# Taking the maximum of the next head's score pair first in each group of VectorE's attention stream

## The reference, cut to what matters

```python
xn = rms_norm(x, gamma)
qkv = xn @ w_qkv                      # 16 heads of 64
q = q * scale
sim = jnp.einsum('bhid,bhjd->bhij', q, k)   # 2048 x 2048 for each head
attn = jax.nn.softmax(sim, axis=-1)
out = jnp.einsum('bhij,bhjd->bhid', attn, v)
return out @ w_out
```

## Time and profile before

| what | value |
|---|---|
| median of 3 runs | 2193.35 us (2187.97 to 2199.1) |
| the profiled execution's own time | 2188.44 us |
| its span | 2186.7 us |
| PE busy | 2024.6 us (93%) |
| DVE busy | 1846.7 us (84%) |
| ACT busy | 1524.8 us (70%) |
| POOL busy | 1416.0 us (65%) |

### The profile page before, as it was taken

One profiled execution on the slowest core, in us unless ns is written; L12 is line 12 of the kernel. 1 busy time (PEld: TensorE's weight loads), 2 busy tenths in 40 slices (PEclk: granted clock), 3 DMA queues, 4 the chain that ended last, 5 costly groups with the idle time before them and its releaser, 6 DMA issues. The chain is left out here.

```text
span 2186.7 us, 25774 instructions
## 1 busy us (share of the span) xinstructions
PE 2024.6 (93%) x8352; PEld 1443.5 (66%) x8352; DVE 1846.7 (84%) x1997; ACT 1524.8 (70%) x1877; POOL 1416.0 (65%) x660
## 2 busy tenths in 40 slices
PE   5999738999868999999999999999999999999887
PEld 4777527777645766767676676676667667666554
DVE  5888785887567899899889889989988998999785
ACT  4666425665425788788788778878878787887764
POOL 1000010000206899899999989989999998999882
PEclk7999857999878999999999999999999999999998
DMA  3310002110050123032130322303223131220000
GB/s 106 75 49 30 0 0 55 49 52 17 0 119 1 42 48 69 16 70 50 41 68 19 68 42 48 68 14 73 43 47 68 18 70 39 48 69 16 6 1 20
DMA packets 77272, 94.68 MB, mean 43 GB/s; under 512 B 31755, under 2 KB 35211, under 8 KB 76870
## 3 DMA queue, kind: packets, MB, share of 16 engines
q1 hardware_dynamic: 77142, 93.04, 18.6%
HBM read 41.11 MB, written 1.42 MB: 19 GB/s over the span
## 5 line engine op out<-in xcount | busy, mean ns | idle before, releaser
L490 POOL TENSOR_TENSOR p_l<-p_raw,p_h 128x1024 fp32r<-128x1024 f32 x512 | 1242.3, 2454 | 140.8 <-ACT p_h L1085 126.7
L1082 ACT ACTIVATE p_raw<-ps 128x1024 f32<-128x1024 f32 x512 | 567.2, 1108 | 234.7 <-PE ps L718 234.1
L1401 DVE TENSOR_REDUCE m_part<-ps 128x1 f32<-128x1024 f32 x480 | 584.5, 1218 | 125.0 <-PE ps L695 124.2
L1085 ACT ACTIVATE p_h<-ps 128x1024 fp32r<-128x1024 f32 x512 | 524.1, 1024 | 0.0
L717 PE MATMUL ps<-qa,ka 128*128 128x512 f32 x1024 | 444.8, 434 | 2.0 <-ACT m_t L1053 2.0
L718 PE MATMUL ps<-qb,kb 65*128 65x512 f32 x1024 | 408.5, 399 | 0.0
L732 PE MATMUL ps<-p_h,v_hl 128*128 128x512 f32 x1024 | 403.1, 394 | 2.3 <-POOL p_l L490 2.2
L1395 DVE TENSOR_REDUCE l_sum<-p_raw 128x128 f32<-128x1280 f32 x256 | 377.1, 1477 | 0.4
L695 PE MATMUL ps<-ka,qa 128*128 128x512 f32 x960 | 315.1, 409 | 12.7 <-DVE m_part L1401 12.3
L735 PE MATMUL ps<-p_l,v_hl 128*64 128x512 f32 x1024 | 320.8, 394 | 0.0
L1381 DVE TENSOR_REDUCE p_raw<-p_raw 128x128 f32<-128x1024 f32 x256 | 309.0, 1208 | 11.7 <-ACT p_raw L1082 11.7
(11 more groups left out here) (185 smaller groups left out, 2669.2 us busy)
## 6 DMA issues: line engine op xcount, KB each, us to landing
big<-g_scratch SPq DMA_DIRECT2D x64, 256.0 KB, 3.2
xnp<-r_scratch SPq DMA_DIRECT2D x59, 256.0 KB, 3.9
qa<-qk_hi SPq DMA_DIRECT2D x112, 128.0 KB, 2.3
ka<-qk_hi SPq DMA_DIRECT2D x56, 128.0 KB, 2.3
kb<-qk_hi SPq DMA_DIRECT2D x56, 128.0 KB, 2.3
ka<-xnp SPq DMA_DIRECT2D x28, 128.0 KB, 2.3
qb<-xnp SPq DMA_DIRECT2D x28, 128.0 KB, 2.4
ka<-qk_low SPq DMA_DIRECT2D x28, 128.0 KB, 3.6
```

The costliest lines, as they stand in the source:

```text
L490: nc.gpsimd.tensor_tensor(p_l[:, g % 4, :, :], slots(g), p_h[:, g % 4, :, :].bitcast(fp32), ALU.subtract).then_inc(pl_done, 1)
L1082: af(slots(g), s_t, ACT.Exp).then_inc(raw_done, 1)
L1085: af(p_h[:, g % 4, :, :], s_t, ACT.Exp).then_inc(ph_done, 1)
L1401: nc.vector.tensor_reduce(m_part[:, it, half:half + 1], ps[:, 4:6, :].rearrange("p b n -> p (b n)"), AX.X, ALU.max).then_inc(s_max, 1)
```

## The change

In each group, VectorE's maximum moves ahead of the sum piece and of the other pieces of that group:

```diff
@@ main_chunk of VectorE
                 for g in range(GROUPS):
+                    for _ in range(PAIRS_OF_MAXIMA[c][g] if has_next else 0):
+                        maximum(head + 1, next(pairs))
                     if g >= GROUPS // 2:
                         first_half_sum(head, c, g - GROUPS // 2)
                     elif exists(summed[0]):
                         whole_sum(*summed, g)
...
                         if g == END_SCALE:
                             end_scale(c)
-                    for _ in range(PAIRS_OF_MAXIMA[c][g] if has_next else 0):
-                        maximum(head + 1, next(pairs))
```

## The result

The changed kernel is slower: 2404.12 us median (2401.21 to 2417.16, 4 runs) against 2190.66 (2186.41 to 2199.1, 4 runs), a ratio of 1.098 with a 95% interval of [1.094, 1.102]. The forecast was 2376, with a range of 2320 to 2430. The profiled execution took 2401.21 us, 212.8 more than the one of before.

The account below looks back on a forecast made before the run. TensorE, busy 1336.0 of 1350 us in the attention, was taken to bound the kernel. Later VectorE pieces add 153 us to the profiled 2188.4, giving 2341.6; 35 us of lower clock makes 2376, range 2320 to 2430.

Parts of the forecast that it names:

- The chain of 0.67 + 1.13 + 1.13 and a tail: VectorE in a group: maximum starts 0.67 us after the score pair, sum piece and last piece each 1.13 later, then TensorE resumes.
- (3, 4): Chunk 3, group 4: column sums wait for the low half, 2.26 us more in each of 14 windows, 31.6 us.
- (3, 6): Chunk 3, group 6: TensorE starts 3.74 us after the pair, 2.36 us more in 14 windows, 33.0 us.
- The first half of a chunk: Whole sum pieces and addition come behind the maxima: chunks 2 and 3 lose 0.78 and 0.68, chunk 1 gains 0.2; 18.9 us.
- (0, 3): Chunk 0, group 3: the value matmul waits for a later low half; 13 us taken, ends 0 and 17.2.
- Edits at nothing: Later reciprocal, low-half DMAs and sum pieces that ScalarE waits for: covered, so no time added.
- The clock: TensorE in the attention: granted clock falls to 0.50 behind the new chunk 3 pauses; 35 us, ends 0 and 106.
- (3, 7): Chunk 3, group 7: the projection waits for the addition, 2.27 us more in 14 windows, 31.8 us.
- the clock stays up: Rival: TensorE's clock does not fall behind the new pauses; 2342 us, chance 0.22.
- longer falls: Rival: in chunk 3 a clock fall may last until the close-following pauses are over; some 2435 us, chance 0.10.
- The faster rival: Rival: the maxima alone of VectorE's work set the pace, so TensorE's pairs start earlier; 2162 us, chance 0.03.
- the pieces stay covered: Rival: something else makes TensorE late at the five places, so pauses replace others; 2190 us, no change, chance 0.05.

Follow-up runs that it names:

- e5: Kernel of before with the maximum moved first only in chunk 3, group 4; 2231.45 us median, ratio 1.017.
- e6: Kernel of before with the maximum moved first only in groups 0 to 3 of chunks 1 to 3; 2245.44 us median, ratio 1.023.
- e2: Kernel of before with only the sum piece moved behind the maximum, all other pieces left ahead of it; 2193.59 us median, ratio 1.0001.
- e4: Changed kernel with eight more matmuls, results unused, ahead of TensorE's waits in groups 4, 6 and 7 of chunk 3; 2354.56 us median, ratio 1.074.
- e1: Kernel of before with the maximum moved first in only five of 31 groups; 2390.89 us median, ratio 1.090.
- e3: Kernel of before with the maximum moved behind the sum piece but ahead of the other pieces; 2281.07 us median, ratio 1.041.

## Why the prediction was right, point by point

*What bounds the kernel.* Right: TensorE had no slack, so every pause was paid in full. In e5 one pause in each of 14 windows, 2.3 us lost each time, made the kernel at least those 32 us longer.

*The chain of 0.67 + 1.13 + 1.13 and a tail.* Right to 0.03 us at (3, 4): 3.77 for 3.74. At (3, 6) the same (1190.72 − 1186.94 = 3.78 after its pair). At (1, 5) 3.23 for 3.14. The lag of 0.06 was 0.10 (1180.40 behind the low half's end at 1180.30), some 0.04 us in some 70 places, 3 us.

*The first half of a chunk.* Right in mechanism and, for chunk 2, in size (12.71 for 12.72). By the starts of the score pairs, averaged over 14 windows, chunk 2 loses 0.71 us, chunk 3 0.66, and chunk 1 gains 0.26, for the 0.78, 0.68 and 0.2 put in. e6's 52 us came out by the same arithmetic for another order, though partly by luck: by the same measure chunk 2 lost 1.55 us there for the 1.91 expected, and chunk 3 2.01 for 1.80.

*(0, 3).* Of the size that was taken: its row in PE's waits has 15.5 us for the 13 put in.

*Edits at nothing.* The later sum pieces, borne out by e2. The later reciprocal and low-half DMAs in the changed order were not tried apart; no wait for them shows among PE's waits.

*The clock.* Right that it would fall behind pauses of this size, and undersized: 35 us, where e4 gives 49.6. By place it was less exact than the total. At (3, 4), 14 falls of 1.5 us make 22 us for the 15 put in. At (3, 6), 14 of 1.3 make 18 for the 5.6 put in: the fall there was priced at 0.6 because TensorE soon waits for VectorE again, but it delays the pair from which VectorE's chain starts, and in 12 of 14 windows it slows that pair too. At (3, 7) five falls make 8 for 15. At (1, 5), put at nothing, three make 5. These are 53 us, the 49.6 and what the two falls left in e4 cost. The price at (3, 6) is the largest miss, some 12 of the 28 us between 2376 and 2404; the total came out nearer than its terms because (3, 7) was too high, which is luck. Of the ends of the clock's term, 0 and 106, the measured value lies in the middle, and the rivals "the clock stays up" and "longer falls" are out: no fall in the changed kernel's windows with maxima lasted longer than the 3.4 us of the first line of the earlier trace rows; in e1 one of 33 did. (In the last window, which has no maxima, falls last 6.8 us. The kernel before has one there too, at 2058 us, so that its clock was at 1.00 up to where the earlier trace rows end and not throughout.) The section of the Trainium skill that the prediction set against it (TensorE: Matmul & The Clock Gate, "HAM oscillation — how this bites in real kernels") names only longer pauses as the danger. The trace doesn't agree: pauses of 2.23 us were enough in all 28 cases of the changed kernel, if not in every one of the others.

*The faster rival* and *the pieces stay covered*: against both stand the five rows of waits. The 2.3 us by which the prediction calls a piece late there is what is lost, not the lateness: the low half of (3, 4) ends 3.67 us after its pair, before 1.15, so it is late by 2.52, of which 0.33 was covered.

The sum without the clock was 153 us; the filled kernel's 2354.56 is 161 above the 2193.12 it was compared with. Of the 8 us between, the lag has 3, (0, 3) another 2.5, and the two falls left in it 3. By the starts of the score pairs TensorE also gets to the next pair 0.1 us later than its late start explains at (3, 6) and at (3, 7), 3 us, and the first halves of the chunks took 2 less than put in. That makes 9 or 10 for 8, within the noise of the medians.

## What to carry to other kernels

When two engines feed each other through a single buffer, an instruction of an in-order engine that waits for its partner should stand behind all that the partner will ask for next, not ahead of it: the work displaced is late by the wait and by its own length, and the wait is not shortened. Before moving a waiting instruction forward, list what the other engine waits for from the pieces it passes, with the cover that each has; here, in chunk 3, the covers were 0.33 to 0.95 us and the pieces came 2.5 us later or more. And an engine that sets the pace pays for a pause a second time where it loses its clock behind it.

## What the runs showed of the hardware that I had not expected

- Matmuls without use made the kernel faster: 336 of them, 49.6 us (e4). Half of them did nearly as well (2362.83 against 2354.56, intervals overlapping).
- A fall of the clock on an engine that is about to wait anyway was not cheap: 0.8 to 1.6 us for one of 3.4 us, because the matmuls up to the pair that starts the partner's chain, and mostly that pair too, ran at 1.2 GHz.
- Pauses of the same 2.23 us at (3, 4) brought the clock down in all 14 windows of the changed kernel, in five of e5 and in two of e1; those of 1.7 us at (1, 5) did so in three of 15 in the changed kernel and in seven in e1. Pauses of up to 1.1 us (e3) and of 1.3 us (e6, and chunk 3 of the kernel with four added matmuls) never did.
